# An attention and expert layer on one core: weight loads moved to SyncE's queue, combining steps placed anew with two of them fused, beta added early, and the last denominators spread by TensorE

## The reference

```
xn = layernorm(x)                                   # x: 4 batches x 1024 tokens x 128, float32

# attention, 16 heads of 64, causal
normed = xn / max(norm(xn), 1e-12) * sqrt(128) * gamma_a
q, k, v = split(normed @ w_qkv)                     # w_qkv: 128 x 3072
sim  = (q / 8) @ k.T ;  sim = where(j > i, -max, sim)
att  = softmax(sim) @ v  -> (tokens, 1024) @ w_out  # w_out: 1024 x 128

# experts: 8 of them, the best 2 of each token
logits = xn @ Wr.T + br ;  w = softmax of the two largest
o_e = relu(xn @ W1[e].T + b1[e]) @ W2[e].T + b2[e]  # 128 -> 512 -> 128
t   = xn + sum of w * o_e over the two
ffn = (t - mean) * rsqrt(var + 1e-5) * gamma_f + beta_f

out = x + att + ffn
```

## Time and profile before

| | |
|---|---|
| median of three runs | 1444.88 us (1441.52 to 1445.03) |
| the profiled execution: own time, span | 1440.34 us, 1438.6 us |
| mean granted clock of TensorE | 0.983 of full speed |
| PE busy | 1360.5 us (95%) |
| DVE busy | 1102.6 us (77%) |
| ACT busy | 1046.0 us (73%) |
| POOL busy | 940.8 us (65%) |

### The profile page before, as it was taken

How to read it: one execution, slowest core, us unless ns; L and a number is a source line. 1 busy time by engine, 2 the same in 40 slices (tenths; PEclk the granted TensorE clock), 3 DMA queues, 4 the chain that set the end, 5 groups by cost and what they waited for, 6 DMA issues and landing times.

```text
span 1438.6 us, 26847 instructions
## 1 busy us (share of the span) xinstructions
PE 1360.5 (95%) x8618; PEld 1017.9 (71%) x8618; DVE 1102.6 (77%) x1944; ACT 1046.0 (73%) x2571; POOL 940.8 (65%) x933
## 2 busy tenths in 40 slices
PE   2789999899999999999999999999999999999996
PEld 2778999566777676767677767677767676767674
DVE  5756666569877987798869886988698869886974
ACT  1556666587877777778777877787877787778774
POOL 1676000387668766876687668766876687668775
PEclk9789999899999999999999999999999999999998
DMA  9132231121212121212121212121212122212212
GB/s 337 42 102 83 62 92 52 45 64 46 51 46 69 45 52 42 70 43 51 40 71 43 50 40 69 45 51 40 70 44 51 42 67 48 51 46 65 49 46 78
DMA packets 80377, 89.87 MB, mean 62 GB/s; under 512 B 17736, under 2 KB 58992, under 8 KB 80240
## 3 DMA queue, kind: packets, MB, share of 16 engines
q1 hardware_dynamic: 59168, 69.90, 19.2%
q10 hardware_dynamic: 16976, 9.86, 2.2%
q0 software_dynamic: 4096, 8.40, 2.0%
HBM read 37.25 MB, written 16.78 MB: 38 GB/s over the span
## 4 chain that ended last, share of the span: by engine, by line
PE 55%; DVE 21%; POOL 3%; issue 2%; ACT 1%; DMA 1%; POOLq 0%; ACTq 0%
PE max_ps L1472 8%; PE score_ps L1497 7%; PE score_ps L1498 7%; PE head_ps L1525 7%; DVE row_max L1329 7%; PE head_ps L1514 6%; PE head_ps L1516 6%; PE misc_ps L1535 3%; DVE x_row L1342 3%; DVE q_a L1319 3%; PE misc_ps L1453 2%; DVE k_b L1319 2%; POOL p_lo L1243 2%; PE max_ps L1475 2%; DVE heads L1384 2%; PE score_ps L1500 2%
## 5 line engine op out<-in xcount | busy, mean ns | idle before, releaser
L1243 POOL TENSOR_TENSOR p_lo<-probs,p_hi 128x512 fp32r<-128x512 f32 (+3 forms) x768 | 797.2, 1057 | 291.1 <-ACT p_hi L1281 288.1
L1281 ACT ACTIVATE probs<-score_ps 128x512 f32<-128x512 f32 (+3 forms) x768 | 376.7, 491 | 180.9 <-PE score_ps L1500 100.0
L1329 DVE TENSOR_REDUCE row_max<-max_ps 128x1 f32<-128x1024 f32 x508 | 383.5, 756 | 153.0 <-PE max_ps L1475 148.8
L1281 ACT ACTIVATE p_hi<-score_ps 128x512 fp32r<-128x512 f32 (+3 forms) x768 | 376.6, 490 | 0.0
L1497 PE MATMUL score_ps<-q_a,k_a 128*128 128x512 f32 (+3 forms) x768 | 287.2, 374 | 2.4 <-ACTq L1250 1.5
L1525 PE MATMUL head_ps<-p_lo,v_hi 128*65 128x512 f32 (+3 forms) x768 | 276.1, 360 | 1.1 <-POOL p_lo L1243 1.1
L1514 PE MATMUL head_ps<-p_hi,v_hi 128*65 128x512 f32 (+3 forms) x768 | 274.8, 358 | 0.0
L1498 PE MATMUL score_ps<-q_b,k_b 65*128 65x512 f32 (+3 forms) x768 | 267.0, 348 | 0.0
L1516 PE MATMUL head_ps<-p_hi,v_lo 128*64 128x512 f32 (+3 forms) x768 | 258.3, 336 | 0.0
L1472 PE MATMUL max_ps<-k_a,q_a 128*128 128x512 f32 x764 | 230.6, 356 | 19.8 <-DVE row_max L1329 18.9
L1472 PEld LDWEIGHTS max_ps<-k_a,q_a 128*128 128x128 f32 x764 | 130.2, 190 | 71.5 <-DVE row_max L1329 43.5
(11 more groups left out here) (190 smaller groups left out, 2171.5 us busy)
## 6 DMA issues: line engine op xcount, KB each, us to landing
k_a<-k_a SPq DMA_DIRECT2D x64, 256.0 KB, 4.0
q_b<-q_a SPq DMA_DIRECT2D x64, 256.0 KB, 4.2
scale<-inv_rows SPq DMA_DIRECT2D x128, 128.0 KB, 2.8
sorted_x<-zeros SPq DMA_DIRECT2D x13, 384.0 KB, 11.6
sorted_y<-result ACTq DMA_DIRECT2D x78, 64.0 KB
w_raw<-sorted_x SPq DMA_DIRECT2D x25, 192.0 KB, 2.4
acc<-in_L_attn_x_dram SPq DMA_DIRECT2D x4, 512.0 KB, 8.1
w_raw<-in_L_ffn_W_dram ACTq DMA_DIRECT2D x4, 512.0 KB, 12.7
```

Source lines behind the costliest of these rows:

```text
L1243: pool.tensor_tensor(p_lo[:, slot, 0:w], probs[:, n_chunk(g, c) % PROBS, 0:w], p_hi[:, slot, 0:w].bitcast(F32), ALU.subtract).then_inc(p_s ...
L1281: ins = act.activation(p[:, n_chunk(g, c) % ring, 0:width], score_ps[n_chunk(g, c) % 2][:, 0:width], ACT.Exp, scale=SCALE)
L1329: dve.tensor_reduce(row_max[:, g % 2, t:t + 1], src, axes, ALU.max).then_inc(max_taken, 1)
```

## The change

- **Loads.** ACT keeps the small parameters and the first two transfers of `w1`. SP issues the rest between the two parts of the zeros: x, six transfers of zeros, all of `w2`, two of `w1`, seven transfers of zeros, the attention weights, `b2`, and the experts' gamma and beta, which it loaded at the start of the second block before.
- **Combining.** `scale`, `gamma`, `beta` and `sum` (seven instructions) become four `gamma` steps, (x - mean) * gamma, and four `sum` steps, x * rstd + acc, each on one tile. There are 37 steps now. `COMBINE_IN` is a table of numbers that gives them other places.
- **Beta** is added to `acc` by POOL in the first block, eight instructions on four tiles each.
- **The last half head.** For the second half of head 63 alone, PE multiplies the denominators with a row of ones, which spreads them to 64 rows in PSUM, and DVE inverts those 64x512 numbers. The three transfers of that half are gone. The last pair's first `y` stands ahead of it.
- **Output.** It is stored in eight transfers of 256 KB, not four of 512 KB.

```diff
@@ block 1, SP
-                    qkv_weights(sp, 0)
-                    sp.wait_ge(set_up, 1)
-                    for r in range(REGIONS):
-                        for i in range(ZERO_CUT[r], ZERO_CUT[r + 1]):
...
+                    sp.wait_ge(set_up, 1)
+                    zero(0)
+                    for i in range(4):
+                        sp.dma_start(w2_parts[i], w2_src[:, 2 * i:2 * i + 2]).then_inc(w2_loaded[i], 16)
+                    for i in range(2, 4):
+                        sp.dma_start(w1_parts[i], w1_src[:, i * 2 * FT:(i + 1) * 2 * FT]).then_inc(w1_loaded[i], 16)
+                    zero(1)
+                    qkv_weights(sp, 0)
+                    sp.dma_start(b2_all[:], b2.partition_broadcast(P)).then_inc(b2_loaded, 16)
+                    sp.dma_start(fgamma[:], ffn_gamma.partition_broadcast(P)).then_inc(small2_loaded, 16)
+                    sp.dma_start(fbeta[:], ffn_beta.partition_broadcast(P)).then_inc(small2_loaded, 16)
@@ block 1, POOL, behind nT_lo
+                    pool.wait_ge(small2_loaded, 32)
+                    for g in range(ALL_GROUPS):
+                        toks = slice(g * GROUP, (g + 1) * GROUP)
+                        pool.tensor_tensor(acc[:, toks], acc[:, toks], fbeta[:].unsqueeze(1).broadcast_to(
+                            [P, GROUP, D]), ALU.add).then_inc(beta_added, 1)
@@ block 1, ACT
-                    for i in range(4):
+                    for i in range(2):
                         act.dma_start(w1_parts[i], w1_src[:, i * 2 * FT:(i + 1) * 2 * FT]).then_inc(w1_loaded[i], 16)
-                    w2_src = w2.rearrange("e d f -> d e f")
-                    for i in range(4):
-                        act.dma_start(w2_parts[i], w2_src[:, 2 * i:2 * i + 2]).then_inc(w2_loaded[i], 16)
-                    act.dma_start(b2_all[:], b2.partition_broadcast(P)).then_inc(b2_loaded, 16)
@@ block 2, the list
-                       + [("scale", q) for q in range(GROUP)] + [("gamma", 0), ("beta", 0), ("sum", 0)])
+                       + [("gamma", q) for q in range(GROUP)] + [("sum", q) for q in range(GROUP)])
-            COMBINE_AT = [(g, c) for g in (3, 4, 5, 6, 7) for c in (0, 1, 4, 6, 8, 9, 10, 11)][:COMBINE_STEPS]
+            COMBINE_IN = {2: (6, 8, 11), 3: (0, 1, 2, 5, 6, 7, 8, 11), 4: (0, 4, 5, 6, 7, 10),
+                          5: (1, 4, 5, 6, 7, 8, 9, 11), 6: (0, 4, 5, 11), 7: (0, 1, 2, 4, 6, 8, 9, 11)}
+            COMBINE_AT = [(r, c) for r in sorted(COMBINE_IN) for c in COMBINE_IN[r]]
...
+            last, pair = ALL_HEADS - 1, ALL_PAIRS - 1
+            order += [("y", pair, 0), ("add", pair, 0), ("broadcast", last, 1), ("invert_wide", last, 1),
+                      ("normalise", last, 1), ("y", pair, 1), ("add", pair, 1)]
@@ block 2, DVE
+                            ins = dve.scalar_tensor_tensor(out=one, in0=one, scalar=gmom[:, q, 0:1], in1=fgamma[:],
+                                                           op0=ALU.subtract, op1=ALU.mult)
...
+                            ins = dve.scalar_tensor_tensor(out=acc[:, tile], in0=one, scalar=gvar[:, 1, q:q + 1],
+                                                           in1=acc[:, tile], op0=ALU.mult, op1=ALU.add)
...
+                        elif kind == "invert_wide":
+                            dve.wait_ge(den_broadcast, 1)
+                            dve.reciprocal(scale[:, c], max_ps[0:HEAD, c]).then_inc(wide_inverted, 1)
@@ block 2, PE
+                        elif kind == "broadcast":
+                            pe.wait_ge(raw_out, n_half(g, c) + 1)
+                            pe.matmul(max_ps[0:HEAD, c], k_b[1][1][HEAD:HEAD + 1, 0:HEAD].bitcast(F32),
+                                      raw[HEAD:HEAD + 1, g % 2, c], start=True, stop=True).then_inc(den_broadcast, 1)
```

More of the change, by code:

```diff
@@ L101, in attention_and_experts @@
         CONSTS0, CONSTS = 5, 8
+        fgamma = sb(whole, "fgamma", [P, D])
+        fbeta = sb(whole, "fbeta", [P, D])
         CUT = [0, 12, ALL_TILES]
@@ L187, in attention_and_experts @@
         nT_lowered = sem("nT_lowered")
+        beta_added = sem("beta_added")
+        den_broadcast = sem("den_broadcast")
+        wide_inverted = sem("wide_inverted")
         waited = sem("waited")
@@ L384, in _, with zero @@
                                      x_tiles[:, b * TILES:(b + 1) * TILES]).then_inc(x_loaded[b], 16)
-                    qkv_weights(sp, 0)
-                    sp.wait_ge(set_up, 1)
-                    for r in range(REGIONS):
+                    w1_src = w1.rearrange("e (f p) d -> p (e f) d", p=P)
+                    w2_src = w2.rearrange("e d f -> d e f")
+                    def zero(r):
                         for i in range(ZERO_CUT[r], ZERO_CUT[r + 1]):
@@ L1088, in beside @@
                 p, since = (g - 2) // 2, (g % 2) * CH + c
-                if 0 <= p < ALL_PAIRS and since in Y_AT:
+                if 0 <= p < ALL_PAIRS - 1 and since in Y_AT:
                     order.append(("y", p, Y_AT[since]))
@@ L1096, in beside @@
                 for kind, lag in CHAIN:
-                    if at >= lag and (at - lag) // CH < ALL_HEADS and (at - lag) % CH in LAST:
+                    if (at >= lag and (at - lag) // CH < ALL_HEADS and (at - lag) % CH in LAST
+                            and at - lag != ALL_HEADS * CH - 1):
                         order.append((kind, (at - lag) // CH, LAST.index((at - lag) % CH)))
@@ L1214, in _ @@
                     for p in range(BATCH):
[L1215 to L1218, removed]
+                        for n in range(2):
+                            t0 = p * TILES + n * GROUP
+                            sp.wait_ge(y_added, n_y((PAIRS - 1) * BATCH + p, n) + 3)
+                            sp.dma_start(out_tiles[:, t0:t0 + GROUP], acc[:, t0:t0 + GROUP]).then_inc(stored, 16)
+                    sp.wait_ge(stored, 16 * 2 * BATCH)
                 @block.gpsimd
@@ L1331, in _ @@
                     summed = [0]
+                    added = [0]
                     def combine(hp, part):
@@ L1360, in combine @@
                             ins = rsqrt_step(dve, q, gvar[:, 0], gvar[:, 1], gvar[:, 2])
-                        elif step == "scale":
-                            ins = dve.tensor_scalar(one, one, gmom[:, q, 0:1], gvar[:, 1, q:q + 1],
-                                                    ALU.subtract, ALU.mult)
                         elif step == "gamma":
[L1365 to L1369, removed]
-                        else:
-                            toks = slice(hp * GROUP, (hp + 1) * GROUP)
-                            ins = dve.tensor_tensor(acc[:, toks], acc[:, toks], x_row[:], ALU.add)
-                            summed[0] = hp + 1
+                            ins = dve.scalar_tensor_tensor(out=one, in0=one, scalar=gmom[:, q, 0:1], in1=fgamma[:],
+                                                           op0=ALU.subtract, op1=ALU.mult)
+                        else:
+                            if added[0]:
+                                dve.wait_ge(y_added, added[0] + 2)
+                            ins = dve.scalar_tensor_tensor(out=acc[:, tile], in0=one, scalar=gvar[:, 1, q:q + 1],
+                                                           in1=acc[:, tile], op0=ALU.mult, op1=ALU.add)
+                            summed[0] = hp * COMBINE_STEPS + part + 1
                         ins.then_inc(comb_step, 1)
@@ L1382, in normalise @@
                         s = g % 2
-                        dve.wait_ge(scale_spread[half], 16 * g + 16)
+                        if g == ALL_HEADS - 1 and half:
+                            dve.wait_ge(wide_inverted, 1)
+                        else:
+                            dve.wait_ge(scale_spread[half], 16 * g + 16)
                         dve.tensor_tensor(heads[s * HEAD:(s + 1) * HEAD, cols], raw[0:HEAD, s, half], scale[:, half],
@@ L1391, in add_y @@
                         if summed[0]:
-                            dve.wait_ge(comb_step, summed[0] * COMBINE_STEPS)
+                            dve.wait_ge(comb_step, summed[0])
                         dve.tensor_tensor(acc[:, toks], misc_ps[u % 2][:].rearrange("p (t d) -> p t d", t=GROUP),
                                           acc[:, toks], ALU.add).then_inc(y_added, 1)
+                        added[0] += 1
                     dve.sem_inc(pv_done, RING)
```

6 lines of the change are left out of this document (2 added, 4 removed).

## The result

The changed kernel takes 1479.3 us (median of five runs, 1477.46 to 1479.51) against 1444.22 us: a ratio of 1.024 (95% interval 1.0229 to 1.0259), slower by 35 us where 15 us less were forecast. Its profiled execution has 1479.51 us, the one of before 1440.34: 39.2 us more. By the first score product of each head in both traces these are -11.0 us until the first head, +48.7 in the eight rounds, and +1.6 from the last head on.

The account below looks back on a forecast made before the run. In attention PE waits for DVE's late maxima, at most 36 us. Start -10.2, combining -6 and end +1.1 sum to -15.1 us: 1444.9 becomes 1429.8, say 1430 us, range 1414 to 1441 us.

Parts of the forecast that it names:

- the term of r = 2: Head r = 2 of each round: two centre steps come in where POOL also gathers; +0.4 us, between 0 and 1.25.
- the steps lose to POOL: Rival: at r = 2, early r = 3, r = 5 and 7, steps wait one more POOL operation; 1470 us, chance 0.05.
- The 1.9 us a round that would turn the sign: Attention rounds: extra loss beyond the count that would cancel the whole gain, 15.1 / 8, given as 1.3 more losses.
- The start: Before the first head: ACT issues fewer loads, so the router starts earlier and the gain lasts; -10.2 us.
- The other heads: Heads r = 3 to 7 of each round: new step places change the length by -0.7, -0.5, +1.3, -1.55, +0.35 us.
- the steps' -6 us: All eight attention rounds: the fused combining steps in new places save 0.7 us a round, -6 us in all.
- The end: Behind the last head: last multiplication +1.75 us, smaller last store -0.7; in all +1.1, between -2.1 and +1.6.
- The forecast's bounds for the product: At the end: the product spreading the denominators over 512 columns takes between 1.0 and 2.04 us by TensorE's clock.
- The ceiling: Attention, eight rounds: any other order of DVE's work can gain at most 36 us, 4.45 us a round.
- the floors of the earlier trace: Round 2 heads where PE is busy throughout: r = 0 at 19.89 us with projections, r = 7 at 15.26 without.

Follow-up runs that it names:

- one place moved: The changed kernel with one combining step a round moved from r = 2 chunk 8 to r = 3 chunk 4: 1450.41 us, ratio 1.0032.
- The best run: The changed kernel with old step places in r = 3 to 5, new in 6 and 7, product with ones first, gathers spread: 1407.05 us, ratio 0.9742.

## Why the prediction was wrong, point by point

- **The failed step** is the term of r = 2: "two `centre` steps come into a head in which POOL also gathers [...]: +0.4, between 0 and one operation, 1.25". It measured +6.15 us a round, 49 us in all. The size came from r = 5, where a step gets in when POOL's running operation ends; I took that for a rule. It holds where POOL keeps up: in r = 5 of the changed kernel three steps wait for one operation each, as forecast (DVE's rows, then POOL's):

```profile
668.00 1.25 DVE L208 SCALAR_TENSOR_TENSOR gvar<-gvar 128x4 f32<-128x4 f32 x1
669.28 0.94 DVE L209 SCALAR_TENSOR_TENSOR gvar<-gvar 128x4 f32<-128x4 f32 x1
670.25 1.21 DVE L206 TENSOR_TENSOR gvar<-gvar 128x4 f32<-128x4 f32 x1
...
667.70 3.74 POOL L1266 TENSOR_TENSOR p_lo<-probs,p_hi 128x512 fp32r<-128x512 f32 x3 [0.17 <-ACT p_hi L1304]
```

  At r = 2 POOL is behind, and the step at chunk 8 waited until the whole queue was worked off. The queue ran dry only because PE stood still, so the wait became PE's, and the lower clock behind it came on top. For the wait the term allowed one operation at most, for the clock nothing.
- **The trace of before showed it**, in rows that I did not weigh. POOL's timeline at r = 2 and the first `centre` step behind it on DVE's:

```profile
609.48 8.42 POOL L1243 TENSOR_TENSOR p_lo<-probs,p_hi 128x512 fp32r<-128x512 f32 x7
```

```profile
615.67 2.31 DVE L1342 TENSOR_SCALAR x_row<-x_row,mean,rstd 128x128 f32<-128x128 f32 x1
```

  Seven operations without a pause, and three more behind them, to 619.97, against three at r = 5; and a step of 0.35 us that took 2.31, two operations and not one. By the earlier trace rows POOL was busy 19.46 of 20.52 us in that head.
- **The rival "the steps lose to POOL"** named the place, r = 2 and the beginning of r = 3, and the sign, with a time of 1470 us; I gave it 0.05. Its mechanism was sized in single operations, four places of 1.25 us; it was one place of 6.15 us. The 1.9 us a round that would turn the sign are 1.5 such operations, not the 1.3 written there.
- **The Trainium skill** (SBUF — State Buffer, "Who interferes with whom") says that the engine that issues first keeps the shared pair of ports for the whole instruction and blocks the other fully. The trace agrees that the step is blocked. Held for one instruction, as the page puts it, the step would have started at 612.36; it was held over four more and ended at 617.07. The measurement decides.
- **The start** was right: -11.0 us to the first head for -10.2, with no wait for `w2`.
- **The other heads** were right in sign but for r = 3: r = 6 -1.28 (forecast -1.55), r = 4 -0.52 (-0.5), r = 5 +1.25 (+1.3), r = 7 +0.38 (+0.35), r = 3 +0.1 (-0.7). Together they made -0.1 us a round for -1.1, so even without r = 2 the steps' -6 us would not have come. With the gathers spread r = 3 has the -0.7.
- **The end**: +1.6 for +1.1. The inverse took 3.35, not 2.8; the first `y` started 0.8 us later behind the last copy of `raw` than taken; from the last addition to the end it took 2.7 us in place of 3.7. The forecast's bounds for the product, 1.0 and 2.04 us by the clock, are about what the runs show (1.07 at 1.00, 1.96 at 0.50). With the product first, the multiplication starts 3.9 us earlier than in the changed kernel, about 1.8 us of it by the order. Over the traces with this same end the time from the last head on is 30.3 to 32.4 us, so one execution can't tell +1.6 from nothing.
- **The ceiling** of 36 us for the order of DVE's work stood. The best run has r = 2 to 7 at 19.92, 15.62, 20.42, 15.47, 20.20 and 15.62, which is 1.8 us a round above the floors of the earlier trace rows, for 4.45 before. A good part of the gain came from moving POOL's gathers, not DVE's steps.

**What stays open.** How far POOL must be behind. At the four ends that the step missed in the changed kernel, POOL's next operation had had its input for 1.6 to 3.2 us (from the end of ACT's `p_hi` to the end of POOL's operation before); at r = 5, where steps got in, for 0.6. But the step of 2.31 us in the kernel before missed one with 0.6 to 0.7, and `heads` got in behind a gather with 3.4. So that time alone does not decide, and no run here tells which state of the queue does.

## What to carry to other kernels

The price of a wait for a shared resource belongs to a place: "one operation" was true where the other engine keeps up, and where it has a queue the loss was 6.15 us, not 0.4. So look first at how long the other engine runs without a pause there, and count its whole run as the upper bound of the wait. And when a step is held by a backlog, spread the work that makes the backlog before moving the step: moving it gave back 29 of 47 us, spreading the gathers 60.

## What the runs showed of the hardware that was not expected

- A VectorE step on SBUF data can be held over several operations of GpSimd: 5.20 us for 128x4 numbers, 5.33 for two tiles, 6.69 for 64x512, each until GpSimd ran dry. Two others, at the beginning of r = 3, were held for 2.31 us (before) and 2.81 us (one place moved) and let in while GpSimd's next operation followed at once. A maximum, which reads PSUM, took its ordinary 0.96 us at the same place of the kernel before, beside the same run of GpSimd.
- GpSimd makes a pause of 0.16 us ahead of an indirect transfer, and one operation behind it waiting VectorE work got in; work of about the same length without these pauses held `heads` 6.69 us in place of 1.7.
- The reciprocal of 64x512 numbers, read from PSUM, took 3.35 us, where 16x32 from SBUF take 0.33: 6.3 ns for each further column.
- The product with ones took 1.96 us in the changed kernel, with a granted clock of 0.50 (1.2 GHz), behind a `y` ahead of which PE had stood for 2.4 us, and 1.07 us in the last run, at 1.00 (2.4 GHz), where it followed 0.68 us behind the last value product. In the run with the spread gathers PE had stood for 2.07 us ahead of the `y`, and the clock was still 1.00.
- One wait of PE can cost more than its length: in the changed kernel's r = 2, behind 4.8 us of standing, the granted clock was 0.50 and the head's work took 1.4 us more.
